# Node products, norms and output rows computed in windows of four steps inside the gather passes of a GNN kernel

## What is computed

```python
# layer 0, twice: a graph convolution with self-loops
h = x @ W; out = segment_sum(h[src] * dinv[src] * dinv[dst], dst) + b
# layer 1: capsule routing, 8 capsules of 16 features, three rounds
z = l2norm(x)[src]; u = l2norm(x)
for _ in range(3):
    p = softmax(sum(z * u[dst]) per capsule); u = l2norm(segment_sum(z * p, dst) + l2norm(x))
# layer 2: mean over the neighbours, then relu(mean @ W + b)
# layer 3: h = gelu(concat(x[src], edge_attr) @ W1 + b1); agg = segment_sum(h @ W2 + b2, dst)
#          layernorm(x + agg) * gamma + beta
x = x + layer(relu(layernorm(x)))
```

## Time and profile before

| | us |
|---|---|
| median of 3 runs (lowest, highest) | 6544.15 (6538.73, 6548.33) |
| profiled execution | 6538.39 |
| its span | 6536.4 |
| PE, PEld, DVE, ACT, POOL busy | 4074.0, 3311.0, 3097.1, 1128.8, 4483.1 |

### The profile page before, as it was taken

How to read it: one execution, slowest core, us unless ns; L and a number is a source line. 1 busy time by engine, 2 the same in 40 slices (tenths; PEclk the granted TensorE clock), 3 DMA queues, 4 the chain that set the end, 5 groups by cost and what they waited for, 6 DMA issues and landing times.

```text
span 6536.4 us, 106387 instructions
## 1 busy us (share of the span) xinstructions
PE 4074.0 (62%) x24704; PEld 3311.0 (51%) x24705; DVE 3097.1 (47%) x7058; ACT 1128.8 (17%) x2550; POOL 4483.1 (69%) x4723
## 2 busy tenths in 40 slices
PE   2444444444444466666678868844444447999997
PEld 1444444444444355555578868834444444555554
DVE  5222223222222777777788888862222235333335
ACT  1000000000000433333343343320000003222223
POOL 6777775777777377777646546547777765777775
PEclk9755556555555777778799989965555566555555
DMA  3111112111111255555467757731111111111111
GB/s 116 52 52 51 51 52 59 52 51 52 52 52 52 89 163 164 164 163 162 149 209 240 241 175 238 240 95 52 52 52 52 52 42 54 52 52 52 52 52 51
DMA packets 355409, 637.62 MB, mean 98 GB/s; under 512 B 85805, under 2 KB 120762, under 8 KB 354826
## 3 DMA queue, kind: packets, MB, share of 16 engines
q0 software_dynamic: 127936, 263.97, 15.6%
q10 hardware_dynamic: 105408, 191.94, 9.4%
q1 hardware_dynamic: 121994, 181.04, 8.2%
HBM read 500.81 MB, written 135.79 MB: 97 GB/s over the span
## 4 chain that ended last, share of the span: by engine, by line
POOL 60%; issue 23%; PE 6%; DVE 6%; DVEq 2%; SPq 1%; DMA 1%; ACT 1%; POOLq 0%; ACTq 0%
POOL u_parts L581 47%; POOL ring L581 12%; PE ps_sum L650 4%; PE ps_u L683 2%; POOL msg L333 1%; DVE zu L1272 1%; SPq L456 1%; DVE stats L955 0%; DVE h L1084 0%; DVE acc L1061 0%; DVEq L251 0%; DVEq L1061 0%; DVE caps_sq L1188 0%; POOL prob_n L560 0%; DVE onehot L1119 0%
## 5 line engine op out<-in xcount | busy, mean ns | idle before, releaser
L581 POOL DMA_INDIRECT u_parts<-table,src x3136 | 3049.7, 972 | 1169.3 <-issue 954.5
L650 PE MATMUL ps_sum<-msg,onehot 128*128 128x128 f32 x7808 | 1423.9, 339 | 183.2 <-DVE msg L333 81.9
L650 PEld LDWEIGHTS ps_sum<-msg,onehot 128*128 128x128 f32 x7808 | 1230.3, 240 | 587.4 <-issue 320.2
L650 PE MATMUL ps_sum<-u_parts,onehot 128*128 x2928 | 718.4, 427 | 865.2 <-SPq L445 810.6
L650 PE MATMUL ps_u<-u_parts,onehot 128*128 x2928 | 708.2, 423 | 793.3 <-SPq L445 756.1
L650 PEld LDWEIGHTS ps_sum<-u_parts,onehot 128*128 128x128 f32 x2928 | 626.8, 318 | 955.7 <-issue 955.6
L650 PEld LDWEIGHTS ps_u<-u_parts,onehot 128*128 128x128 f32 x2928 | 624.1, 316 | 874.3 <-issue 874.3
L1047 DVE SCALAR_TENSOR_TENSOR onehot<-dst,minus_row,iota 128x512 f32<-128x512 f32 x1220 | 911.2, 748 | 285.8 <-issue 266.8
L581 POOL DMA_INDIRECT ring<-table,src x784 | 789.0, 1006 | 324.2 <-issue 238.6
L1061 DVE TENSOR_TENSOR acc<-ps_sum,acc 128x128 f32 x1342 | 379.0, 282 | 1197.2 <-PE ps_sum L650 1192.9
L683 PE MATMUL ps_u<-u_parts,hots 128*128 x5904 | 493.5, 234 | 304.7 <-ACT hots L853 212.1
(11 more groups left out here) (158 smaller groups left out, 2737.9 us busy)
## 6 DMA issues: line engine op xcount, KB each, us to landing
ring<-z_rows SPq DMA_DIRECT2D x392, 256.0 KB, 3.3
hots<-hot_rows ACTq DMA_DIRECT2D x248, 256.0 KB, 3.3
hot_rows<-hots ACTq DMA_DIRECT2D x244, 256.0 KB
u_parts<-table,src POOLq DMA_INDIRECT x3136, 2.5
z_rows<-ring SPq DMA_DIRECT2D x196, 256.0 KB
wide<-hot_rows ACTq DMA_DIRECT2D x120, 256.0 KB, 3.2
wide_t<-hot_rows ACTq DMA_DIRECT2D x120, 256.0 KB, 3.6
ring<-table,src POOLq DMA_INDIRECT x784
```

What stands on the lines that cost most here:

```text
L581: nc.gpsimd.indirect_dma_start(out=slot(p, c % slots)[:, t * P:(t + 1) * P], out_offset=None, in_=tables[p], in_offset=bass.IndirectOffset ...
L650: last = nc.tensor.matmul(sums[k % len(sums)][:, 0:P], lhsT=onehot[:, k % HOTS, t, :], rhs=rows(t), start=(t == 0), stop=(t == TILES - 1))
```

## The change

**Windows.** The 244 steps are cut into 61 windows of four. The four steps of a window can have touched at most four blocks, beginning with the block of its first step. Some steps behind each window all engines do the node work of these four blocks, inside the pass, in the bodies of `over_steps`. A block that gets more edges later is done and stored again by the next windows; the last one holds.

**In CONV1, CONV2 and MEAN** VectorE reads the four blocks, scaled, at the age of 6 steps, TensorE transposes at 7 and multiplies at 8, ScalarE copies between, VectorE adds bias and scales at 11. In CONV2 and MEAN it also takes the moments; ScalarE takes the root, applies the norm at 12, and in CONV2 the capsules' lengths follow at 13 and 14, in MEAN the second product (WE) at 13 to 15. ScalarE stores the window's 512 rows into the next table. GpSimd waits for 61 stores where it waited for four cuts.

**In EDGE** the last product is at 7 to 11 (`WO`), the norm with gamma and beta at 11 to 15, and ScalarE stores the window's output rows at 16. The instruction of GpSimd that added beta (L590) becomes one of VectorE ahead of the steps, behind the 52 bias instructions. ScalarE normalizes all rows (52 instructions) ahead of the EDGE steps, where the second node product had normalized them in passing.

**Other moves.** The convolution's second sum runs in `h`, the capsules' sums in `x`. Before CAPS1 SyncE loads the normalized rows back from the table into `h` in four pieces, and the split waits for these. The attributes' product is 128 partitions deep, with zeros behind the 12.

```diff
+WINDOWS = STEPS // UNROLL
-        attr_t = sb("attr_t", [TILES * D_EDGE, 2, P])
+        attr_t = sb("attr_t", [P, 2, P])
-        WE_attr = sb("WE_attr", [TILES * D_EDGE, TILES, P])
+        WE_attr = sb("WE_attr", [P, TILES, P])
+        def on(k, age):
+            return (k - age) % UNROLL == 0
+        def blocks_at(eng, s, age, chunk):
+            at = s.back(age)
+            first = block_of(at, chunk(age))
+            return ds(first if at.fixed else eng.snap(first), GROUP)
...
+                if p == CAPS1:
+                    sp.wait_ge(rows_stored, 16 * WINDOWS * 2)
+                    for q in range(PIECES):
+                        b0, b1 = q * PIECE, min((q + 1) * PIECE, BLOCKS)
+                        sp.dma_start(h[:, b0:b1, :],
+                                     tables[p].rearrange("(b p) f -> p b f", p=P)[:, b0:b1, :])\
+                          .then_inc(h_in[q], 16)
...
-                pool.wait_ge(table_stored, 16 * len(CUTS) * (n + 1))
+                if p in (CONV1, MEAN):
+                    pool.wait_ge(table_stored, 16 * len(CUTS) * (1 if p == CONV1 else 2))
+                else:
+                    pool.wait_ge(rows_stored, 16 * WINDOWS * (CONV2, CAPS1, EDGE).index(p) + 16 * WINDOWS)
...
-            pool.wait_ge(slot_free, CHUNKS * EDGE + 1)
-            nc.gpsimd.tensor_tensor(x[:, :, :], x[:, :, :], BT[:, :].unsqueeze(1).to_broadcast([P, NB, P]),
-                                    ALU.add).then_inc(beta_added, 1)
...
+            def plain_pass(p, m, weights):
                 def body(s, k, chunk, have):
...
+                    if on(k, 7) and have(7):
+                        turn(s, m, 7)
+                    if on(k, 8) and have(8):
+                        multiply(s, m, 8, weights)
+                    if p == MEAN and on(k, 13) and have(13):
+                        turn_rows(s, 13)
+                    if p == MEAN and on(k, 14) and have(14):
+                        multiply_rows(s, 14)
...
+            def read_window(s, m, p, age, into):
+                at = s.back(age)
+                dve.wait_ge(step_added, at + (STEPS * p + UNROLL))
+                if m or not starts(s, age):
+                    dve.wait_ge(win_turned, at + STEPS * m)
+                into(win_in).then_inc(win_read, UNROLL)
+                dve.wait_ge(win_read, at + (STEPS * m + UNROLL))
...
+            def conv2_window(s, k, chunk, have):
+                if on(k, 6) and have(6):
+                    win = blocks_at(dve, s, 6, chunk)
+                    read_window(s, 1, CONV2, 6,
+                                lambda into: V.tensor_tensor(into, h[:, win, :], rows(dinv, win), ALU.mult))
+                if on(k, 11) and have(11):
+                    win = blocks_at(dve, s, 11, chunk)
+                    product = biased(s, 1, 11, B2)
+                    V.tensor_tensor(acc[:, win, :], x[:, win, :], product, ALU.add).then_inc(win_out, UNROLL)
+                    window_moments(s, 1, 0, 11, acc[:, win, :])
+                if on(k, 12) and have(12):
+                    window_scales(s, 0, 12, blocks_at(dve, s, 12, chunk))
...
+            dve.wait_ge(blocks_normed, NORMED[3])
             for b in range(NB):
-                last = V.scalar_tensor_tensor(out=h[:, b, :], in0=BO[:, :], scalar=deg[:, b:b + 1],
+                last = V.scalar_tensor_tensor(out=x[:, b, :], in0=BO[:, :], scalar=deg[:, b:b + 1],
...
+            link(V.tensor_tensor(h[:, :, :], h[:, :, :], BT[:, :].unsqueeze(1).to_broadcast([P, NB, P]),
+                                 ALU.add))
...
+                if on(k, 15) and have(15):
+                    V.tensor_tensor(win_sum, win_h, per_feature(GA, GROUP), ALU.mult)\
+                     .then_inc(win_biased, UNROLL)
...
+                    V.tensor_tensor(win_rows, win_sum, h[:, win, :], ALU.add).then_inc(win_rows_ready, UNROLL)
...
+                if on(k, 8) and have(8):
+                    copy_turned(s, 3, 8)
+                if on(k, 12) and have(12):
+                    root_window(s, 2, 12)
+                if on(k, 14) and have(14):
+                    norm_window(s, 2, 14, win_y, slice(0, GROUP), ACT.Identity)
+                if on(k, 16) and have(16):
+                    win = blocks_at(act, s, 16, chunk)
+                    store_window(s, out.rearrange("p (b f) -> p b f", f=P)[:, win, :], win_rows,
+                                 win_rows_ready, s.back(16) + (2 * STEPS + UNROLL))
```

More of the change, by code:

```diff
@@ L38 @@
 assert NB % PIECES == 0 and PIECES == 4
+assert GROUP == UNROLL and BLOCKS - 1 + GROUP <= NB
 assert STEPS <= 256 and CHUNKS <= 2 * P
@@ L417, in _ @@
                 loads = p in (CAPS2, CAPS3)
-                if not loads:
-                    source = h if p in (CAPS1, MEAN) else acc
+                if p in (CONV1, MEAN):
+                    source = acc if p == CONV1 else h
                     for i, (g0, g1) in enumerate(CUTS):
@@ new lines, in turn, with multiply @@
+            def turn(s, m, age):
+                at = s.back(age)
+                pe.wait_ge(win_read, at + (STEPS * m + UNROLL))
+                if m or not starts(s, age):
+                    pe.wait_ge(win_copied, at + STEPS * m)
+                for t in range(GROUP):
+                    last = nc.tensor.transpose(ps_a[:, t * P:(t + 1) * P], win_in[:, t, :], ident[:, :])
+                last.then_inc(win_turned, UNROLL)
+            def multiply(s, m, age, weights):
+                at = s.back(age)
+                pe.wait_ge(win_copied, at + (STEPS * m + UNROLL))
+                if m or not starts(s, age):
+                    pe.wait_ge(win_out, at + STEPS * m)
+                for t in range(GROUP):
+                    last = nc.tensor.matmul(ps_b[:, t * P:(t + 1) * P], lhsT=win_t[:, t, :],
+                                            rhs=weights[:, :], start=True, stop=True)
+                last.then_inc(win_mm, UNROLL)
@@ new lines, in copy_rows, with root_window @@
+            def copy_rows(s, age):
+                at = s.back(age)
+                act.wait_ge(row_turned, at + UNROLL)
+                if not starts(s, age):
+                    act.wait_ge(row_mm, at + 0)
+                nc.scalar.activation(row_t.rearrange("p t f -> p (t f)"), ps_c[0][:, :], ACT.Copy)\
+                  .then_inc(row_copied, UNROLL)
+            def root_window(s, n, age):
+                at = s.back(age)
+                act.wait_ge(win_var, at + (STEPS * n + UNROLL))
+                nc.scalar.activation(small[:, 2, 0:GROUP], small[:, 2, 0:GROUP], ACT.Sqrt)\
+                  .then_inc(win_root, UNROLL)
@@ new lines, in norm_window @@
+            def norm_window(s, n, age, source, cols, func):
+                at = s.back(age)
+                act.wait_ge(win_moments, at + (STEPS * n + UNROLL))
+                for t in range(GROUP):
+                    last = nc.scalar.activation(win_h[:, t, :], source[:, t, :], func,
+                                                bias=shift_cols[:, cols, :][:, t, :],
+                                                scale=rstd_cols[:, cols, :][:, t, :])
+                last.then_inc(win_normed, UNROLL)
```

481 lines of the change are left out of this document (271 added, 210 removed).

## The result

The changed kernel takes **6473.17 us** (median of 4, 6467.09 to 6477.16), the kernel before, run beside it, 6541.44 (median of 4, 6531.74 to 6548.33). The ratio is 0.9891, 95% interval 0.9879 to 0.9903: 1.1% faster. The forecast was 6478, in a range of 6420 to 6595. The profiled execution took 6477.16 us, its span is 6475.4, that of the one before 6536.4.

The account below looks back on a forecast made before the run. GpSimd's gathers were taken to set the passes and node work the gaps: 6538.4 less 170.5 saved plus 104 lost gave 6472 for the profiled execution; the median, 5.8 higher, was forecast at 6478, range 6420 to 6595.

Parts of the forecast that it names:

- CONV1, CONV2, MEAN longer: In these three passes the windows' VectorE instructions would hold gathers, costing 22, 32 and 25 us.
- EDGE's pass, start included: EDGE's gathers would lose 10 us to the windows and 12 us to the start.
- the three gaps: Gaps CONV1 to CONV2, CONV2 to CAPS1, MEAN to EDGE would shrink to 19.6, 34.5 and 32.6 us.
- The tail: Behind EDGE's last gather, 22.8 us would remain in place of 70.3, saving 47.5.
- The gathers' holds: In the passes, VectorE instructions with two SBUF inputs would delay gathers, 0.12 us for each such window instruction.
- EDGE's one-hots: In EDGE, one-hots falling in phase with the landings would take 12 us off the windows' cost of 22.
- The start of CAPS1: Eight subtractions among CAPS1's first gathers would hold them 3 us more; one-hots would begin 23 us behind the first gather.
- the ring: Buffered gathers would cover the later one-hots: 28 gathers, 35 us, in CAPS1; 56 gathers, 70 us, in EDGE.
- The start of EDGE: The 52 bias instructions and beta's addition, falling among EDGE's first gathers, would hold them 12 us more.
- Rival A: In the passes, windows would hold gathers longer; 0.64 us a window cancels the gain, up to 6637 us; chance 0.11.
- Rival B: EDGE would be paced by TensorE at 1.2 GHz, 19.0 us a window, giving 6624 us; chance 0.12.
- Rival C: Windows would cost the gathers nothing, only the two starts' 15 us being lost: 6389 us; chance, with values near it, 0.07.

Follow-up runs that it names:

- a_start: The changed kernel with the constants of EDGE's 52 bias instructions and of beta's addition over all blocks read from PSUM; 6457.30 us, ratio 0.9882.
- a_k12: The changed kernel with the attributes' product 12 partitions deep again in place of 128, run on chip B; 7672.74 us, ratio 1.0205.
- a_best2: The changed kernel with the one-hots' iota, windows' constants and EDGE's start constants in PSUM, and EDGE's root one step later; 6329.52 us, ratio 0.9689.
- b_iota: The kernel before with the one-hots' iota read from PSUM in CONV1, CONV2, CAPS1 and EDGE, MEAN kept on SBUF; 6457.03 us, ratio 0.9879.
- a_iota: The changed kernel with the one-hots' iota read from PSUM except in MEAN; 6420.07 us, ratio 0.9825.

## Why the prediction was right, point by point

| term | foretold | measured |
|---|---|---|
| gap CONV1 to CONV2 | 19.6 | 17.4 |
| gap CONV2 to CAPS1 | 34.5 | 37.1 |
| gap MEAN to EDGE | 32.6 | 33.7 |
| tail | 22.8 | 45.9 |
| saved by these | 170.5 | 145.9 |
| CONV1, CONV2, MEAN longer | 22, 32, 25 | 29.8, 24.7, 11.5 |
| EDGE's pass, start included | 22 | 20.3 |
| start of CAPS1 | 3 | -0.1 |
| lost by these | 104 | 86.2 |

The forecast for the profiled execution was 6472, its time 6477. That is closer than the terms deserve: the gaps gave 24.6 less and the passes took 17.8 less, two errors that cancel by luck.

- **What bounds it, the three gaps.** Right, each within 2.6 us. A drain of two windows, counted from durations of the kernel before, was enough.
- **The tail.** The worst step of the sum. I took EDGE's windows to be paced by gathers and the last addition to come 6 us behind the last gather. I had checked that TensorE's sum (under 10 us of 16.8) and ScalarE's sum of work fit into a window, and no chain: the order add, Gelu, root, copy, product, with two buffers, and the slow products behind each wait take 17.07. Busy sums per engine were right (TensorE's is 10.5) and didn't answer the question. Of the 23.1 us that the tail is longer than foretold, 20.9 are this lag; 2.2 are the drain behind the last addition, 19.0 for 16.8. In a version with free gathers it costs what these would give.
- **The gathers' holds.** The mechanism was right and is now shown, not only argued: a second input in PSUM takes the hold to zero. The value of 0.12 us an instruction stood for values between 0.03 (MEAN's read) and 0.23 (gamma): it is a mean over phases, good for a sum over many, not for one pass. Gamma's is on the edge between nothing and 0.52: in a_start its gathers begin a little later, at 0.049 us and more, and it took 28.1 us in place of 14.3. MEAN was priced at over twice what it cost for that reason, CONV1 at three quarters.
- **EDGE's one-hots** fell from 37.5 to 22.9; I had taken off 12. In the same pass gamma and beta took 22.6, and I had put down 22 with the copy and the small ones.
- **The start of CAPS1.** Its subtractions held the gathers 2.4 us more, near the 3 foretold, and its one-hots began 26.3 us behind the first gather (23 foretold), which the ring covered. That the pass came out even is the messages' holds, 7 us less, against the one-hots', 4 more.
- **The start of EDGE.** Foretold 12 us more; the held time rose by 9.9 and, by a_start, 9.4 us of the held 17 are in the time. The two gathers took 12.29 and 6.83 us.
- **Rival A** needed 0.64 us a window; CONV1, the worst, has 0.49. **Rival B**: a_k12 shows on chip B that TensorE's low clock would have come back without the zero rows, at a price of 86 to 94 us there. From the ratios (1.0205 over 1.0072 or 1.0080, times 0.9891) I estimate 1.001 to 1.002 of before on the first chip: the gain gone, and less than the rival's 6624. **Rival C** is out in the changed kernel. It is, in CONV1 and CONV2, what a_best2 makes true by other means: 978 us a pass, windows and all.

Rival C stood on a rule of the Trainium skill. Its page SBUF — State Buffer, section Who interferes with whom, infers that a tensor_tensor does not stall DMA descriptor generation. Here 38 gathers beside one window's read in CONV1 were held 13.0 us, and the hold vanished when one input moved to PSUM. For a gather the measurement decides against the inference. But the prediction also read the rule's other half too narrowly. A gather's row names `src`, its row numbers, as an input, and they lie in SBUF; so it is itself an instruction that reads SBUF, and with such an instruction, says the same section of the Trainium skill's page SBUF — State Buffer, a VectorE instruction with two SBUF inputs does contend. The same 38 gathers agree with that half, and by it the windows would never have been free. Which part of a gather waits, no run shows.

## What to carry to other kernels

Before moving work beside a paced stream, ask what it shares with the stream: here two inputs from SBUF on VectorE against GpSimd's gathers, which one constant in PSUM removes, at no cost that the runs show. Price the drain of a pipeline from durations, but price its pace from the chain through the engines' queues and buffers, not from each engine's busy sum, and count the products behind a wait at the low clock. And a gain that rests on slack in a loop is a gain only where the slack is: on a chip where the loop had none, the change's nearest relatives lost.

## What the runs showed of the hardware that I had not expected

- For an instruction with two inputs the hold is all or nothing by operand place: 784 gathers in CONV1 of b_iota with 0.02 us of excess beside one-hots, 12.9 before, from one input of one instruction.
- A hold lasts for what is left of the VectorE instruction: 0.43 us for gathers that begin 0.14 us into a 0.69 us add, 0.38 at 0.19 us.
- Short two-input instructions back to back hold one gather through the whole train: 12.29 us in the changed kernel, 8.29 before.
- An instruction with one SBUF input (EDGE's scaled copy of a window, 0.43 us for 512 columns in place of 0.69) holds a little too: 4.4 us in 28 gathers of a_iota, 0.16 each.
- Zero rows in a product changed the granted clock of a stretch, from 0.55 to 0.76 on chip B with the windows, and EDGE had 0.50 before and 0.79 after on the first; a 12-row product of the same 512 columns ran at 1.2 GHz throughout.
- With the same 52 records a window, TensorE's clock behind a wait made windows of 15.5 to 17.0 us.
- Two chips run the same kernel 15% apart, with gathers and packets of the same length on both; on the slow one the semaphore updates for finished sums come late and in bursts.
